# Both feed-forward networks of a hybrid block: the down projection two tiles behind the up projection, ScalarE's copy with fewer waits, and the running sum of squares on GpSimd

## The chip, the cores and the metric

The kernel runs on one core of one Trainium2 chip. The core has TensorE (PE) for matmuls, VectorE (DVE) and ScalarE (ACT) for elementwise work, GpSimd (POOL), and SyncE (SP), which here only issues transfers. Each engine runs its own instructions in the order in which they are written and waits for the others through semaphores. The metric is the device time of one execution in microseconds, as the median of several runs.

## The reference, cut to what matters

The whole block is four residual steps on `x` of 8 x 512 rows by 256 columns: attention, a feed-forward network (FFN), a recurrent scan, and the same FFN once more with the same weights. The FFN is this:

```
def _ternary_linear(x, w):
    alpha = jnp.mean(jnp.abs(w))
    w_t = jnp.sign(w) * (jnp.abs(w) > 0.5 * alpha).astype(w.dtype)
    rms = jnp.sqrt(jnp.sum(x * x, axis=-1, keepdims=True)) / jnp.sqrt(x.shape[-1])
    return jnp.einsum('bsd,fd->bsf', x / (rms + 1e-8), w_t)     # (forward value)

h = jax.nn.gelu(_ternary_linear(layernorm(x), w_up), approximate=False)    # 256 -> 1024
x = x + _ternary_linear(h, w_down)                                         # 1024 -> 256
```

So each FFN needs gelu of an up projection, the down projection of that, and for each row the sum of the squares of its 1024 values of `h`, by which the result is scaled.

## The kernel before, in words

`x` stays in SBUF through all four steps. An FFN (`ffn_pe`, `ffn_act`, `ffn_dve`, `ffn_pool`, one function for each engine, called with i = 0 for the first FFN and i = 1 for the second) goes over 8 **batches** q of 512 rows. Within a batch it goes over NF = 8 **tiles** n of 128 hidden features; t = 8q + n numbers all tiles. All of an FFN's matrices of one tile are 128 partitions (features) by 512 columns (rows of x).

For one tile t these steps are done:

- TensorE, `up` (L267): 4 matmuls of 512 columns, fp16 weights with the high and the low half of `x` (`xh`), into PSUM bank 2 or 3 in turn. It waits until ScalarE's gelu of tile t-2 has read that bank (semaphore `g`).
- ScalarE: gelu from the bank into `h` (L322, fp32, two buffers), a copy scaled by 2^7 and rounded to fp16 into `hh[..., 0]` (L327), and the square into `hsq` (L328, two buffers). Before the gelu it waits for `up` of t, and for VectorE's low half of t-2 (`hl`), which reads `h`. Before the copy it waits for the down projection of t-2 (`dnm`), whose `hh` buffer it writes, and for the sum that reads the `hsq` buffer (`ss`); the square comes after the copy.
- VectorE: the low half `hh[..., 1]` = h * 2^7 - hh[..., 0] (L413), and from n = 1 on, the running sum of squares `ssq` (L425, 7 additions a batch).
- TensorE, `down` (L282): 8 matmuls of 256 columns with `hh` of both halves as weights, which add up in PSUM over the 8 tiles.

TensorE's order within a batch is up(t), down(t-1), up(t+1), down(t), and so on. `square_sums` (L291: 8 passes of a matmul against a column of ones) of batch q-1 follows at n = 1, and the transposes of the next batch's rows (`turned_rows`, L240) at n = 2 and 3.

VectorE has, beside L413 and L425, work for the neighbouring batches, written out by hand tile by tile: at n = 0 the scales and the normalised rows of the next batch (L357 to L367), at n = 1 to 3 the layernorm statistics of the batch after it (L343 to L353), at n = 4 and 5 the low half of the next `xh` (L251), at n = 2 the reading of the square sums of the batch before (L373), at n = 4 the scale from them (L377, L379), at n = 4 to 6 the residual additions (L386), and in the first FFN at n = 6 and 7 the statistics for the layernorm of the scan (L394 to L403). GpSimd takes only small powers: the root of the square sums (`output_roots`, L465), the roots of the variances (`row_roots`, L255), and once in the first FFN L478.

SyncE's queue stores each finished batch in the second FFN (L532), after `x` is complete.

Of the kernel before, what the change touches and what calls it, by code (L numbers as in the profile page):

```python
# [34 lines left out]
P = 128  # L35
# [49 lines left out]
def build(nc, a_in, out):  # L85
    with ExitStack() as ctx:
# [3 lines left out]
        def sb(name, shape, dt=F32, where=ctx):  # L90
            return where.enter_context(nc.sbuf_tensor(name, shape, dt))
# [65 lines left out]
        mid.close()  # L157
        xh = sb("xh", [P, 2, 2, KD, L], F16, mid)
        h = sb("h", [P, 2, L], F32, mid)
        hh = sb("hh", [P, 2, 2, L], F16, mid)  # L160
        hsq = sb("hsq", [P, 2, L], F32, mid)
        ssq = sb("ssq", [P, 3, L], F32, mid)
        ysc = sb("ysc", [P, 4, NT], F32, mid)
# [93 lines left out]
        def ffn_pe(pe, i):  # L257
            def up(q, n):
                t = q * NF + n
                if n == 0:  # L260
                    pe.wait_ge(F["hi"], q * KD + KD)
                    pe.wait_ge(F["lo"], q * KD + KD)
                if t >= 2:
                    pe.wait_ge(F["g"], t - 1)
                for part in range(2):
                    for k in range(KD):
                        last = pe.matmul(bank[2 + n % 2][:, :], wup[:, k, n * P:(n + 1) * P], xh[:, q % 2, part, k, :],  # L267
                                         start=(part == 0 and k == 0), stop=(part == 1 and k == KD - 1))
                last.then_inc(F["up"], 1)

            def down(t):
                q, e = divmod(t, NF)
                pe.wait_ge(F["hh"], t + 1)
                pe.wait_ge(F["hl"], t + 1)
                if e == 0 and q >= 2:
                    pe.wait_ge(F["x"], (q - 1) * NT)
                if e == 0 and q in (B, B + 1):
                    pe.wait_ge(O["t"], (2 * NT - 1) * B - 2 * (B + 1 - q))
                    pe.wait_ge(Z["sq"], B - 2 * (B + 1 - q))
                for u in range(NT):  # L280
                    for part in range(2):
                        last = pe.matmul(bank[4 + q % 2 * 2 + u // 2][:, u % 2 * D:u % 2 * D + D],  # L282
                                         hh[:, t % 2, part, u * P:(u + 1) * P], wdn[:, e, :],
                                         start=(e == 0 and part == 0 and u % 2 == 0), stop=(e == NF - 1 and part == 1),
                                         skip_group_check=True)
                last.then_inc(F["dnm"], 1)

            def square_sums(q):
                pe.wait_ge(F["ss"], q * (NF - 1) + NF - 1)
                for u in range(NT):  # L290
                    last = pe.matmul(bank[0][:, u:u + 1], ssq[:, (q * (NF - 1) + NF - 2) % 3, u * P:(u + 1) * P], ones[:, 0:1],  # L291
                                     start=True, stop=True, skip_group_check=True)
                last.then_inc(F["sm"], 1)

            if i == 0:
                pe.wait_ge(w_q, 2)
                pe.wait_ge(A["x2"], B * NT)
                for k in (1, 0):
                    turned_rows(pe, 0, k)
            for q in range(i * B, i * B + B):  # L300
                for n in range(NF):
                    up(q, n)
                    if q > i * B or n > 0:
                        down(q * NF + n - 1)
                    if n == 1 and q > i * B:
                        square_sums(q - 1)
                    if n in (2, 3) and q < i * B + B - 1:
                        turned_rows(pe, q + 1, 3 - n)
            down((i * B + B) * NF - 1)
            square_sums(i * B + B - 1)  # L310

        def ffn_act(act, i):
            if i == 0:
                for k in (1, 0):
                    high_half(act, 0, k)
            for q in range(i * B, i * B + B):
                for n in range(NF):
                    t = q * NF + n
                    act.wait_ge(F["up"], t + 1)
                    if t >= 2:  # L320
                        act.wait_ge(F["hl"], t - 1)
                    act.activation(h[:, t % 2, :], bank[2 + n % 2][:, :], ACT.Gelu, scale=1.0 / HI_X).then_inc(F["g"], 1)  # L322
                    act.wait_ge(F["g"], t + 1)
                    if t >= 2:
                        act.wait_ge(F["dnm"], t - 1)
                        act.wait_ge(F["ss"], q * (NF - 1) + max(n - 2, min(n, 2) - 1))
                    act.activation(hh[:, t % 2, 0, :], h[:, t % 2, :], ACT.Copy, scale=HI_H).then_inc(F["hh"], 1)  # L327
                    act.activation(hsq[:, t % 2, :], h[:, t % 2, :], ACT.Square).then_inc(F["sq"], 1)  # L328
                    if n in (3, 4) and q < i * B + B - 1:
                        high_half(act, q + 1, 4 - n)  # L330
# [39 lines left out]
        def ffn_dve(dve, i):  # L370
# [38 lines left out]
            for q in range(q0, q9 + 1):  # L409
                for n in range(NF):  # L410
                    t = q * NF + n
                    dve.wait_ge(F["hh"], t + 1)
                    dve.scalar_tensor_tensor(hh[:, t % 2, 1, :], h[:, t % 2, :], HI_H, hh[:, t % 2, 0, :],  # L413
                                             ALU.mult, ALU.subtract).then_inc(F["hl"], 1)
                    if n >= 1:
                        s = q * (NF - 1) + n - 1
                        dve.wait_ge(F["sq"], t + 1)
                        if n == 1:
                            old = hsq[:, 1 - t % 2, :]
                        else:  # L420
                            old = ssq[:, (s - 1) % 3, :]
                            dve.wait_ge(F["ss"], s)
                        if n == 3:
                            dve.wait_ge(F["sm"], q)
                        dve.tensor_tensor(ssq[:, s % 3, :], old, hsq[:, t % 2, :], ALU.add).then_inc(F["ss"], 1)  # L425
                    if i == 0 and n == 0 and q == 3:
                        dve.wait_ge(C["mc"], 2)
                        dve.tensor_scalar(tile_columns(0), mean_b[:, 0:B * NT:NT, 1], LN_EPS, None, ALU.add).then_inc(C["ve"], 1)
                    if i == 0 and n == 0 and q == 5:
                        dve.wait_ge(C["rs"], 1)  # L430
                        dve.scalar_tensor_tensor(tile_columns(2), mean_b[:, 0:B * NT:NT, 0], -1.0, tile_columns(1),
                                                 ALU.mult, ALU.mult).then_inc(C["nm"], 1)
                    if q < q9:
                        if n == 0:
                            row_scales(dve, q + 1)
                            rows_normalised(dve, q + 1, range(NT))
                        if n in (4, 5):
                            low_half(dve, q + 1, 5 - n)
                    if q + 1 < q9:
                        if n in (1, 2):  # L440
                            row_stats(dve, q + 2, (2 * n - 2, 2 * n - 1))
                        if n == 3:
                            row_moments(dve, q + 2)
                    if q > q0:
                        if n == 2:
                            read_sums(q - 1)
                        if n == 4:
                            output_scales(q - 1)
                        if n in (4, 5, 6):
                            add_rows(q - 1, ((0,), (1, 2), (3,))[n - 4])  # L450
                        if i == 0 and n in (6, 7):
                            next_stats(q - 1, (2 * n - 12, 2 * n - 11))
                        if i == 0 and n == 7:
                            next_moments(q - 1)
# [7 lines left out]
        def ffn_pool(pool, i):  # L462
            def output_roots(q):
                pool.wait_ge(F["sr"], q + 1)
                pool.tensor_tensor(ysc[:, 1, :], ysc[:, 0, :], halves[:, 0, :], ALU.pow).then_inc(F["s1"], 1)  # L465
# [3 lines left out]
                row_roots(pool, 0)  # L469
                row_roots(pool, 1)  # L470
            for q in range(q0, q9 + 1):
                if q > q0:
                    output_roots(q - 1)
                if q + 1 < q9:
                    row_roots(pool, q + 2)
                if i == 0 and q == 3:
                    pool.wait_ge(C["ve"], 1)
                    pool.tensor_tensor(tile_columns(1), tile_columns(0), inverse[:, :, 0], ALU.pow).then_inc(C["rs"], 1)  # L478
            output_roots(q9)

        block = ctx.enter_context(nc.Block())
# [1400 lines left out]
```

## Time and profile before

| | value |
|---|---|
| median of 3 runs | 2365.93 us (2363.47 to 2369.75) |
| the profiled execution: time, span | 2368.05 us, 2366.3 us |
| granted TensorE clock, mean over the span | 0.836 of full |
| busy share of the span: PE, DVE, ACT, POOL | 77%, 89%, 70%, 40% |
| first FFN: first `up` to last reading of the square sums | 488.4 to 645.7 us |
| second FFN: the same | 2206.3 to 2359.6 us |

The two FFNs stand at the two ends of the recurrent scan, in which VectorE is busy nearly all of the time. An FFN's time is best read as a period: L373 runs once a batch, so the distance from one L373 to the next is the time of one batch of 8 tiles. Durations of a row contain a tail during which the next instruction of the same engine already runs; the distance from start to start says what an instruction costs its engine.

### The profile page before, as it was taken

Reading aid. Unit: us, or ns where it says so; the run is one execution under the profiler, and the core shown is the slowest. Engines: PE = TensorE matmul, PEld = TensorE weight load, DVE = VectorE, ACT = ScalarE, POOL = GpSimd, SP = SyncE. Lnnn points to the kernel's source line nnn. Section 1 sums busy time; section 2 is a strip of 40 time slices with the busy share of each in tenths; the row PEclk is TensorE's granted clock in tenths of the full one; section 3 lists DMA queues with packets and bytes.
Section 4 is the critical chain, followed back from the end, with each engine's and each line's share of the span. In section 5 each row is a group of like instructions: output and inputs, shape, how many; then the busy total and the mean of one; then the engine's idle time right before and its main releaser. Section 6 shows DMA issues by size and latency. Waiting matters only on the chain.

```text
span 2366.3 us, 47628 instructions
## 1 busy us (share of the span) xinstructions
PE 1824.5 (77%) x12321; PEld 1478.2 (62%) x12321; DVE 2117.0 (89%) x9102; ACT 1656.0 (70%) x5481; POOL 956.6 (40%) x1608
## 2 busy tenths in 40 slices
PE   5888888788888777877777788877877877343887
PEld 3555555455587666777777777777766777342654
DVE  6888777679817999999999999999999999999887
ACT  4878888667746666667777777777777666555776
POOL 0000000001005666666665666666666555666110
PEclk8999899889997888788888777888778777666999
DMA  6000000000000000000000000000000000000001
GB/s 189 18 18 22 18 18 18 13 1 1 1 1 1 1 1 1 1 1 1 2 1 1 1 1 2 1 1 1 1 1 1 1 1 1 1 1 1 10 28 36
DMA packets 14351, 25.00 MB, mean 11 GB/s; under 512 B 1280, under 2 KB 12032, under 8 KB 13824
## 3 DMA queue, kind: packets, MB, share of 16 engines
q1 hardware_dynamic: 14080, 21.97, 3.2%
q8 instruction: 99, 1.62, 0.3%
q14 instruction: 172, 1.41, 0.2%
HBM read 12.27 MB, written 4.19 MB: 7 GB/s over the span
## 4 chain that ended last, share of the span: by engine, by line
DVE 63%; PE 14%; issue 13%; ACT 5%; POOL 0%; DVEq 0%; POOLq 0%; ACTq 0%
DVE xs L1581 9%; DVE pn L1561 8%; DVE bank L1565 8%; DVE U L1630 7%; DVE bank L1595 7%; DVE pn L1586 6%; DVE kv L1619 5%; PE bank L282 3%; PE bank L267 3%; ACT prob L923 2%; PE bank L585 2%; DVE bank L1603 2%; DVE bank L1615 1%; PE bank L632 1%; PE bank L669 1%
## 5 line engine op out<-in xcount | busy, mean ns | idle before, releaser
L750 PE MATMUL bank<-U,ident 128*128 128x128 f32 x2048 | 463.5, 398 | 159.6 <-ACT go L1064 140.1
L750 PEld LDWEIGHTS bank<-U,ident 128*128 128x128 f32 x2048 | 430.1, 257 | 195.5 <-issue 162.3
L1779 POOL TENSOR_TENSOR wu<-U,stg 128x256 f32<-128x256 f32 x512 | 317.7, 620 | 561.3 <-DVE U L1630 561.3
L1253 ACT ACTIVATE xs<-U 128x128 f32<-128x128 f32 x1024 | 261.4, 301 | 304.1 <-DVE U L1630 301.4
L761 PE MATMUL bank<-stack,tm 128*128 128x64 f32 x1792 | 273.8, 324 | 110.1 <-ACT tm L994 100.4
L761 PEld LDWEIGHTS bank<-stack,tm 128*128 128x128 f32 x1792 | 263.7, 237 | 127.5 <-ACT tm L994 115.8
L1708 POOL TENSOR_TENSOR kv<-stg 128x256 f32<-128x256 f32 x513 | 317.4, 619 | 0.0
L1581 DVE TENSOR_TENSOR xs<-U,bank 128x128 f32<-128x128 f32 x1024 | 243.5, 278 | 62.1 <-ACT bank L1107 61.1
L1565 DVE TENSOR_TENSOR bank<-wu,bank 128x128 f32<-128x128 f32 x1024 | 290.0, 283 | 1.8 <-POOL wu L1779 1.4
L735 PE MATMUL bank<-wcat,yT 128*128 128x224 f32 x1024 | 275.9, 425 | 5.8 <-issue 5.4
L1595 DVE TENSOR_TENSOR bank<-pn,bank 128x128 f32<-128x128 f32 x1024 | 248.3, 288 | 1.1 <-issue 0.8
L1630 DVE TENSOR_TENSOR U<-bank,kv 128x128 f32<-128x128 f32 x1024 | 246.6, 281 | 2.4 <-issue 1.7
L735 PEld LDWEIGHTS bank<-wcat,yT 128*128 128x128 f32 x1024 | 228.0, 233 | 28.4 <-issue 18.8
L1561 DVE TENSOR_REDUCE pn<-xs 128x8 f32<-128x128 f32 x1026 | 241.0, 275 | 0.2 <-ACT xs L1253 0.2
L1586 DVE TENSOR_REDUCE pn<-xs 128x8 f32<-128x128 f32 x1024 | 238.9, 274 | 0.0
L923 ACT ACTIVATE prob<-bank,nmax 128x128 f32<-128x128 f32 x512 | 180.5, 371 | 48.7 <-DVE nmax L1369 48.1
L282 PE MATMUL bank<-wdn,hh 128*128 128x256 f16 x1024 | 133.3, 273 | 41.0 <-DVE hh L413 31.3
L1155 ACT ACTIVATE small<-pn 128x16 f32<-128x16 f32 x513 | 110.8, 216 | 75.2 <-DVE pn L1561 33.0
L1619 DVE TENSOR_TENSOR kv<-bank,kv 128x256 f32<-128x256 f32 x384 | 159.6, 416 | 0.5
L994 ACT ACTIVATE tm<-bank 64x448 f32<-64x448 f32 x256 | 136.0, 531 | 32.8 <-PE bank L761 27.1
L282 PEld LDWEIGHTS bank<-wdn,hh 128*128 128x128 f16 x1024 | 92.9, 97 | 102.2 <-issue 64.2
L1369 DVE TENSOR_REDUCE nmax<-bank 128x4 f32<-128x512 f32 x128 | 87.7, 685 | 67.7 <-PE bank L620 67.2
(213 smaller groups left out, 3708.0 us busy)
## 6 DMA issues: line engine op xcount, KB each, us to landing
out_x<-x SPq DMA_DIRECT2D x8, 512.0 KB, 2.9
x<-in_x SPq DMA_DIRECT2D x1, 3584.0 KB, 16.9
Vs<-V SPq DMA_DIRECT2D x8, 384.0 KB, 4.6
Vs<-V SPq DMA_DIRECT2D x8, 288.0 KB, 3.3
lane<-in_lanes SPq DMA_DIRECT2D x8, 256.0 KB, 3.2
wcat<-in_wcat SPq DMA_DIRECT2D x1, 1792.0 KB, 14.5
wraw<-in_w_up SPq DMA_DIRECT2D x1, 1024.0 KB, 19.0
wraw<-in_w_down SPq DMA_DIRECT2D x1, 1024.0 KB, 11.4
```

Of the source, the lines that this page charges most:

```text
L282: last = pe.matmul(bank[4 + q % 2 * 2 + u // 2][:, u % 2 * D:u % 2 * D + D], hh[:, t % 2, part, u * P:(u + 1) * P], wdn[:, e, :], start=(e ...
L735: last = pe.matmul(bank[dst][:, e * PB * H:(e + 1) * PB * H], yT[:, (pc // 2) % 2, k, pc % 2, 4 * g + 2 * e:4 * g + 2 * e + 2, :].rearrang ...
L750: last = pe.matmul(rsum.rearrange("p (t i) -> p t i", i=HD), ident[:, :], steps[:, :, :, j], start=(j == 0), stop=(j == HD - 1))
L761: last = pe.matmul(bank[3 + g][:, e * CH:(e + 1) * CH], tm[:, g * (PB // 2) + e, :, :].rearrange("p a c -> p (a c)"), stack[:, :], start=T ...
L1561: dve.tensor_reduce(pn[:, e, 1, :], ij(xs[:, e, 1, :]), AXX, ALU.add).then_inc(S["ps"], 1)
L1565: dve.tensor_tensor(rows8(zz, e), rows8(wu, e), rows8(zz, e), ALU.subtract).then_inc(T[e]["d"], 1)
L1581: dve.tensor_tensor(ij(xs[:, e, 0, :]), ij(rows8(U[:, half if j else 1 - half, (j - 1) % STEPS, :], e)), row(kkr[:, jj, :], i=HD // 2), AL ...
L1586: dve.tensor_reduce(pn[:, e, 0, :], ij(xs[:, e, 0, :]), AXX, ALU.add).then_inc(T[e]["pn"], 1)
L1595: dve.tensor_tensor(ij(rows8(zz, e)), col(pn[:, e, 0, :], HD // 2), row(kkar[:, g, jj, :], i=HD // 2), ALU.mult).then_inc(T[e]["z"], 1)
L1630: dve.tensor_tensor(rows8(U[:, half, j, :], e), rows8(zz, e), rows8(new, e), ALU.add).then_inc(T[e]["u"], 1)
L1708: pool.tensor_tensor(ij(kv0[:, j % 2, :]), col(stg[:, half, j, TK, :]), row(stg[:, half, j, TV, :]), ALU.mult).then_inc(S["k0"], 1)
L1779: pool.tensor_tensor(ij(wu[:, :]), ij(U[:, half if j else 1 - half, (j - 1) % STEPS, :]), col(stg[:, half, j, TW, :]), ALU.mult).then_inc( ...
```

## The change

The down projection runs two tiles behind the up projection instead of one; `hh` gets a third buffer for it. On ScalarE the copy waits for the down projection of t-3 instead of t-2, and the wait for the running sum moves from before the copy to before the square. The 7 additions a batch that keep the running sum leave VectorE and go to GpSimd, with their waits; GpSimd's roots, which stood at the head of each batch, now follow its additions of n = 3, 5 and 6.

```
-        hh = sb("hh", [P, 2, 2, L], F16, mid)
+        hh = sb("hh", [P, 3, 2, L], F16, mid)
 ... ffn_pe (and hh[:, t % 3 ...] in down)
                     up(q, n)
-                    if q > i * B or n > 0:
-                        down(q * NF + n - 1)
+                    if q > i * B or n > 1:
+                        down(q * NF + n - 2)
 ...
-            down((i * B + B) * NF - 1)
+            for t in (2, 1):
+                down((i * B + B) * NF - t)
             square_sums(i * B + B - 1)
 ... ffn_act
                     if t >= 2:
-                        act.wait_ge(F["dnm"], t - 1)
+                        act.wait_ge(F["dnm"], t - 2)
+                    act.activation(hh[:, t % 3, 0, :], h[:, t % 2, :], ACT.Copy, scale=HI_H).then_inc(F["hh"], 1)
+                    if t >= 2:
                         act.wait_ge(F["ss"], q * (NF - 1) + max(n - 2, min(n, 2) - 1))
-                    act.activation(hh[:, t % 2, 0, :], h[:, t % 2, :], ACT.Copy, scale=HI_H).then_inc(F["hh"], 1)
                     act.activation(hsq[:, t % 2, :], h[:, t % 2, :], ACT.Square).then_inc(F["sq"], 1)
 ... ffn_dve: the block "if n >= 1: ... tensor_tensor(ssq ...)" is gone
 ... ffn_pool
             for q in range(q0, q9 + 1):
-                if q > q0:
-                    output_roots(q - 1)
-                if q + 1 < q9:
-                    row_roots(pool, q + 2)
-                if i == 0 and q == 3:
-                    (L478)
+                for n in range(1, NF):
+                    s = q * (NF - 1) + n - 1
+                    t = q * NF + n
+                    pool.wait_ge(F["sq"], t + 1)
+                    if n == 1:
+                        old = hsq[:, 1 - t % 2, :]
+                    else:
+                        old = ssq[:, (s - 1) % 3, :]
+                        pool.wait_ge(F["ss"], s)
+                    if n == 3:
+                        pool.wait_ge(F["sm"], q)
+                    pool.tensor_tensor(ssq[:, s % 3, :], old, hsq[:, t % 2, :], ALU.add).then_inc(F["ss"], 1)
+                    if n == 3 and q > q0:
+                        output_roots(q - 1)
+                    if n == 5 and q + 1 < q9:
+                        row_roots(pool, q + 2)
+                    if n == 6 and i == 0 and q == 3:
+                        (L478)
```

## Rows read from the trace of the kernel before

**Rows 1.** One batch of each FFN: window, busy by engine (instructions), clock, DMA share, GB/s

```profile
core 0: us, PE busy (x) PEld busy (x) DVE busy (x) ACT busy (x) POOL busy (x), PEclk, DMA share, GB/s
...
555.43:575.31 19.88, 16.82 (x113) 10.54 (x112) 18.08 (x53) 15.01 (x27) 4.55 (x3) 1.00 0.00 1
...
2254.00:2273.00 19.00, 16.56 (x112) 10.61 (x112) 16.20 (x44) 14.76 (x27) 2.64 (x2) 1.00 0.09 29
```

**Rows 2.** Line L373, once a batch: count, duration ns, first and last start

```profile
L373 DVE TENSOR_SCALAR ysc<-bank x16: 143/144/162, 515.7 to 2359.6; 128x4 f32<-128x4 f32 x16
...
L373 DVE TENSOR_SCALAR ysc<-bank x1: 154/154/154, 633.9 to 633.9; 128x4 f32<-128x4 f32 x1
...
L373 DVE TENSOR_SCALAR ysc<-bank x1: 144/144/144, 2234.9 to 2234.9; 128x4 f32<-128x4 f32 x1
...
L373 DVE TENSOR_SCALAR ysc<-bank x1: 154/154/154, 2347.9 to 2347.9; 128x4 f32<-128x4 f32 x1
```

**Rows 3.** Timeline, one tile round in batch 0: start, us, engine, line [idle before]

```profile
503.59 0.60 ACT L322 ACTIVATE h<-bank 128x512 f32<-128x512 f32 x1
...
504.21 0.63 ACT L327 ACTIVATE hh<-h 128x512 f16<-128x512 f32 x1
...
504.75 0.61 ACT L328 ACTIVATE hsq<-h 128x512 f32<-128x512 f32 x1
504.88 0.69 DVE L413 SCALAR_TENSOR_TENSOR hh<-h,hh 128x512 f16<-128x512 f32 x1
...
505.72 1.03 PE L282 MATMUL bank<-wdn,hh 128*128 128x256 f16 x8
...
506.59 1.03 PE L267 MATMUL bank<-xh,wup 128*128 128x512 f16 x4
...
507.65 0.60 ACT L322 ACTIVATE h<-bank 128x512 f32<-128x512 f32 x1
```

**Rows 4.** Waits in the first FFN: who, for whom: us, times, longest

```profile
PEld bank L282 <- issue: 38.7, 49, 1.5
ACT h L322 <- PE bank L267: 33.3, 44, 1.9
...
DVE hh L413 <- ACT hh L327: 19.9, 28, 3.3
```

**Rows 5.** Chain of waits, TensorE back to back at a batch's start: start, us, what

```profile
570.44 0.79 PE bank L291 x8
571.23 0.89 PE bank L267 x4
572.11 0.88 PE bank L282 x8
572.99 0.44 PE bank L240 x4
```

**Rows 6.** Timeline of VectorE over tiles n = 0 and 1 of a batch

```profile
568.62 0.68 DVE L413 SCALAR_TENSOR_TENSOR hh<-h,hh 128x512 f16<-128x512 f32 x1
...
571.12 0.68 DVE L413 SCALAR_TENSOR_TENSOR hh<-h,hh 128x512 f16<-128x512 f32 x1
...
571.72 0.68 DVE L425 TENSOR_TENSOR ssq<-hsq 128x512 f32<-128x512 f32 x1
...
572.32 0.74 DVE L343 BATCH_NORM_STATS2 st<-x 128x6 f32<-128x256 f32 x2
```

**Rows 7.** GpSimd by shape, whole span: count, busy us, mean ns, idle before

```profile
L1731 POOL TENSOR_TENSOR ov<-rs,fac 128x128 f32<-128x128 f32 x65 | 29.6, 456 | 0.8 <-ACT fac L1145 0.8
...
L255 POOL TENSOR_TENSOR sd<-vv,halves 128x8 f32<-128x8 f32 x16 | 26.2, 1638 | 195.4 <-DVE vv L353 195.4
...
L1746 POOL TENSOR_TENSOR y<-y,ln_w 128x256 f32<-128x256 f32 x24 | 17.4, 725 | 0.4 <-ACT y L1099 0.4
...
L465 POOL TENSOR_TENSOR ysc<-ysc,halves 128x4 f32<-128x4 f32 x16 | 16.1, 1007 | 239.3 <-DVE ysc L373 239.3
```

**Rows 8.** Timeline, a GpSimd root and VectorE's low half at the same time

```profile
500.59 1.64 POOL L255 TENSOR_TENSOR sd<-vv,halves 128x8 f32<-128x8 f32 x1 [17.35 <-DVE vv L353]
...
500.81 0.69 DVE L413 SCALAR_TENSOR_TENSOR hh<-h,hh 128x512 f16<-128x512 f32 x1 [0.30 <-ACT hh L327]
```

More of the change, by code:

```diff
@@ L282, in down @@
                         last = pe.matmul(bank[4 + q % 2 * 2 + u // 2][:, u % 2 * D:u % 2 * D + D],
-                                         hh[:, t % 2, part, u * P:(u + 1) * P], wdn[:, e, :],
+                                         hh[:, t % 3, part, u * P:(u + 1) * P], wdn[:, e, :],
                                          start=(e == 0 and part == 0 and u % 2 == 0), stop=(e == NF - 1 and part == 1),
@@ L412, in ffn_dve @@
                     dve.wait_ge(F["hh"], t + 1)
-                    dve.scalar_tensor_tensor(hh[:, t % 2, 1, :], h[:, t % 2, :], HI_H, hh[:, t % 2, 0, :],
+                    dve.scalar_tensor_tensor(hh[:, t % 3, 1, :], h[:, t % 2, :], HI_H, hh[:, t % 3, 0, :],
                                              ALU.mult, ALU.subtract).then_inc(F["hl"], 1)
[L415 to L425, printed above, removed]
                     if i == 0 and n == 0 and q == 3:
@@ L471, in ffn_pool @@
             for q in range(q0, q9 + 1):
-                if q > q0:
-                    output_roots(q - 1)
-                if q + 1 < q9:
-                    row_roots(pool, q + 2)
-                if i == 0 and q == 3:
-                    pool.wait_ge(C["ve"], 1)
-                    pool.tensor_tensor(tile_columns(1), tile_columns(0), inverse[:, :, 0], ALU.pow).then_inc(C["rs"], 1)
+                for n in range(1, NF):
[15 more added lines that the diff above has]
+                    if n == 6 and i == 0 and q == 3:
+                        pool.wait_ge(C["ve"], 1)
+                        pool.tensor_tensor(tile_columns(1), tile_columns(0), inverse[:, :, 0], ALU.pow).then_inc(C["rs"], 1)
             output_roots(q9)
```

## The prediction

> **What bounds the kernel now.** I read the page's slices first: the two FFNs are short stages in which all of TensorE, VectorE and ScalarE are at six to nine tenths, so a share of busy time names no bound there. The next view is the busy time by window over exactly one batch, from one L373 to the next [rows 1]. In the first FFN a batch takes 19.88 us, VectorE is busy for 18.08 of them, TensorE for 16.82, ScalarE for 15.01. In the second it takes 19.00 us with VectorE at 16.20. So VectorE is nearly the bound in the first FFN and not in the second, which is hardly faster: something else holds both. The granted clock is 1.00 in both windows, which is the 2.4 GHz level.
>
> The starts of L373 [rows 2] give the mean period: from 515.7 to 633.9 are six batches, 19.7 us each; from 2234.9 to 2347.9 six batches, 18.83 us each.
>
> The timeline of one round shows the second limit [rows 3]. Gelu of tile t starts at 503.59, the copy at 504.21, VectorE's low half at 504.88, the down projection at 505.72, the up projection behind it at 506.59, and only when that is done at 507.62 can the gelu of t+2 start, at 507.65. That is a loop over four engines of 4.06 us for two tiles, 2.03 us a tile, 16.2 us for eight, with every engine idle in part of it. The view of waits says the same [rows 4]: ScalarE's gelu waits 33.3 us for the up projection, VectorE's low half 19.9 us for the copy, and TensorE stands 38.7 us ahead of the down projection. On top of the loop come VectorE's bursts: L413 of n = 0 and that of n = 1 are 2.50 us apart (568.62, 571.12) because the next batch's rows are normalised in between, and L425 follows every one of them [rows 6]. So a batch is partly the loop, partly VectorE's queue in front of L413.
>
> **The floor of each engine after the change.** TensorE: an up projection costs 0.87 us from start to start, a down projection 0.88 (572.11 to 572.99, 505.72 to 506.59), the square sums 0.79, one group of transposes 0.44 [rows 3, 5]. 8 x 1.75 + 0.79 + 2 x 0.44 = 15.7 us a batch. ScalarE issues what it issued, 15.0 us busy [rows 1], and waits for less. VectorE loses 7 additions at 0.60 us from start to start (571.72 to 572.32 [rows 6]), 4.2 us a batch: 18.1 becomes 13.9 in the first FFN, 16.2 becomes 12.0 in the second. GpSimd gains 7 additions of 128x512 from two inputs. The trace has none of that size, so it is extrapolated: 456 ns for 128 columns, 725 for 256 [rows 7], 2.1 ns a column, so 1.26 us for 512. From below the cost is 0.725 us (the 256-column row itself), from above 2.5 us, twice the extrapolation, if something on the way halves its rate. I take 1.26, and 1.33 with the wait of each addition for the one before it, an estimate of 0.07 from the gaps between the rows of [rows 3] (the low half starts 0.04 us after the copy ends). 7 x 1.33 + 1.01 + 1.64 = 12.0 us a batch, under TensorE's 15.7. TensorE is then the bound.
>
> **What each wait is worth then.** *Down two behind.* In TensorE's order, 3.5 us pass (two ups and two downs) between the end of up(t), where gelu(t) starts, and down(t). The low half of t ends 1.98 us after the gelu's start (503.59 to 505.57 [rows 3]), and 0.15 us later the matmul starts (505.72). The slack is 3.5 - 2.1 = 1.4 us, where before it was negative (0.88 + 0.87 - 2.1). The loop over the four engines now spans three tiles for its 2.1 + 0.9 + 1.0 = 4.0 us, 1.35 us a tile, and falls away behind TensorE's 1.75. What is late next is VectorE's queue: at n = 0 the 2.5 us burst delays L413 of n = 1 by about 2.5 - 1.75 = 0.75 us, inside the slack. In the first FFN n = 4 to 7 hold the residual additions and two sets of statistics and come to about 2 us each, so 4 x 0.25 = 1.0 us of delay runs into the burst and makes 1.75, beyond the slack by 0.35. I add 0.4 us a batch there and nothing in the second FFN.
>
> *The copy's waits.* Both waits before the copy hardly cost anything before: the list of waits in the first FFN has one of 0.5 us, in the second none. No gain. The square now carries the wait for the sum of t-2, and behind it on ScalarE stand the next gelu and so the next up projection. With the addition ending 1.16 + 0.61 + 0.08 + 1.26 = 3.1 us after gelu(t) [rows 3, 7] and the square of t+2 starting 3.5 + 1.16 = 4.7 us after it, there is 1.6 us of room. The two roots take it: additions 3, 4, 5, 6 run back to back with 1.01 and 1.64 us between them. 4 x 1.33 + 2.65 + 1.85 = 9.8 us after gelu(3), the sum of n = 6 is done, and the square of the next batch's n = 0 wants it 5 x 1.75 + 1.16 = 9.9 us after gelu(3). That is an even fit, so I add 0.3 us a batch for it in both FFNs; if an addition took 1.5 us it would be 0.7 more.
>
> *Square sums.* TensorE reaches them after down(7) of the batch before, 3.5 + 0.88 us after gelu(7); by the same count the last addition of the batch, behind the roots, ends at 9.8 + 1.33 = 11.1 us after gelu(3), that is 4.1 us after gelu(7). It fits by 0.3 us, and what it costs if not is the whole of the overrun on TensorE's queue. L478 adds 1.9 us once. GpSimd's roots come later than before but VectorE wants L465's result at n = 4 and L255's only in the next batch. SyncE's stores in the second FFN come closer together; they are 0.09 of the DMA engines' time [rows 1], nothing waits for them but the last, which follows the end as before.
>
> **The sum.** A batch comes to 15.7 + 0.4 + 0.3 = 16.4 us in the first FFN and 16.0 in the second. Between the L373 of [rows 2]: 6 x (19.7 - 16.4) = 19.8 us and 6 x (18.83 - 16.0) = 17.0 us. Before the first L373 of an FFN lie ten tiles more, at the loop's 2.03 us a tile: 10 x (2.03 - 1.75) = 2.8 us, of which I take 2.5 for each FFN, 5.0 together. Behind the last one lie five tiles, 1.4 us, less 0.2 at the very end, where the square sums now wait for square and addition (3.1 us after the gelu, and 0.1 for the wait) and not for low half and down (2.13 + 0.88 = 3.0 us): 1.0 with a little lost, 2.0 together. The gain is 19.8 + 17.0 + 5.0 + 2.0 = 43.8 us. The profiled execution took 2368.05 us (span 2366.3 and 1.75 around it), so 2324.2; the median of the runs shown is 2.1 us lower, and I forecast **2323 us**. With every added loss at nothing it would be 15.7 us a batch and about 2314.
>
> **Where VectorE and GpSimd may meet.** Overlap of a large GpSimd operation with a VectorE operation that reads two tensors in SBUF is a resource that the trace shows only in small: L413 reads `h` and `hh`, both in SBUF, and ran from 500.81 for 0.69 us inside a GpSimd root (500.59 for 1.64 us), neither longer than elsewhere [rows 8]. That is the nearest row and I take nothing for it; but the root reads 8 columns and the addition 1024.
>
> The Trainium skill says otherwise ("SBUF — State Buffer", section "Who interferes with whom"): a VectorE instruction with two SBUF inputs and a GpSimd instruction that reads SBUF exclude each other, and whichever issues first holds the pair for its whole length. By that rule L413 of [rows 8] should have started at 502.23; it did not, so for a whole instruction the trace disagrees, but a narrower form of it (while the operands stream) would be open. By it the time would be that of the first rival, 2343 us.
>
> **Rivals.** *1. Low half and addition take turns (0.33).* What it does here: each of the 8 low halves (0.66 us) and 7 additions (1.26) a batch runs alone, with some 0.1 us for each handing over. Lowest sum: 5.3 + 8.8 + 1.5 = 15.6, just TensorE's floor; but VectorE also has 9.1 us of other work a batch in the first FFN (13.9 - 8 x 0.60), and when it comes late to L413 it finds GpSimd inside an addition. In strict turns a tile costs 0.66 + 1.26 + 0.2 = 2.1 us where there is an addition, and n = 0 2.5: 7 x 2.1 + 2.5 = 17.2, and the root's delays bring it to 17.8 in the first FFN, say 17.4 in the second. Gain 6 x 1.9 + 6 x 1.4 + 4 = 24 us: 2368 - 24 - 2 = 2342, say 2343. For it: the addition fills its operands' path for over a microsecond. Against it: [rows 8].
>
> *2. The other side: GpSimd becomes the bound (0.07).* ScalarE's square waits for the addition of t-2, so everything goes at GpSimd's pace once 7 additions and 2.65 us of roots exceed the old period, 7a + 2.65 > 19.2, a > 2.4 us. It decides from there; at 3 us an addition a batch takes 23.7 us and 14 of them cost 4.4 us each, about 60 us, 2425. For it: the extrapolation is from half the width, and VectorE's queue may slow it. Against it: the two widths of [rows 7] put it at half of that.
>
> *3. The period hardly moves (0.07).* The wait for the sums, or another wait before TensorE, takes the place of the loop and a batch stays at 18.5 to 19.5 us: 2355 to 2368, around 2360. For it: four engines between 75 and 100% have little room for each other. Against: no single count above gives over 16.4.
>
> **How the numbers follow.** The forecast, 2314 to 2332, has 0.53, rival 1 (2334 to 2352) 0.33, rival 3 0.07, rival 2 0.07. A measurement of this kernel tells from no change what is over 0.3%, 7 us. Faster: 0.53 + 0.33 and a small part of rival 3, 0.87. Same: 0.06. Slower: 0.07. The range, 2311 to 2351, leaves out rivals 2 and 3 and a little of each end.
>
> **What would show it.** After: no VectorE addition in the FFNs; GpSimd's addition at 1.2 to 1.35 us; the period of L373 near 16.4 and 16.0 us with TensorE's busy time at 15.7 or more of it and no wait over 0.5 us ahead of L282; the gelu waiting for the up projection only. Rival 1 shows as additions and L413 longer than 1.35 and 0.69 us, or starting only when the other ends. Rival 2 shows as ScalarE's square waiting for GpSimd at most tiles. The scan between the FFNs should keep its length to some microseconds; if the whole differs while the FFNs' periods come out as said, the reason lies there. The prediction is wrong if the period stays above 18 us, or if the square sums hold TensorE.

## The result, and the profile after

The changed kernel takes 2353.66 us (median of 6 runs, 2348.46 to 2361.97), the kernel before beside it 2368.14 us (median of 6). The ratio is 0.9942 with a 95% interval of 0.9920 to 0.9964: some 14 us faster. The forecast was 2323 us with a range of 2311 to 2351; the sign was right, the gain was a third of it, and the time lies above the range.

The profiled execution took 2354.65 us (span 2352.5). First, the same two windows of one batch each as in [rows 1] (window, then busy us and instructions of PE, PEld, DVE, ACT, POOL, the granted clock, DMA):

```profile
core 0: us, PE busy (x) PEld busy (x) DVE busy (x) ACT busy (x) POOL busy (x), PEclk, DMA share, GB/s
550.30:570.50 20.20, 16.41 (x112) 10.91 (x112) 18.73 (x47) 15.36 (x29) 14.17 (x11) 1.00 0.00 1
2245.50:2263.90 18.40, 16.25 (x112) 10.99 (x112) 16.54 (x37) 14.58 (x27) 12.65 (x10) 1.00 0.09 30
```

VectorE has 6 or 7 instructions fewer in each window and is busier than before in both (18.73 against 18.08 us, 16.54 against 16.20). Single batches mislead here, though: the first window holds the one batch with L481, GpSimd's extra power, and at 20.2 us it is the longest of the first FFN. Over six batches of each FFN the picture is milder; the first two rows are from the kernel before, the last two from the changed one:

```profile
515.70:633.90 118.20, 99.08 (x664) 62.50 (x665) 103.42 (x294) 88.72 (x157) 16.13 (x12) 1.00 0.00 1
2234.90:2347.90 113.00, 98.08 (x664) 62.85 (x664) 92.40 (x231) 88.48 (x157) 14.22 (x11) 1.00 0.09 29
...
512.60:621.30 108.70, 97.94 (x675) 65.77 (x674) 95.65 (x252) 87.36 (x157) 74.33 (x55) 1.00 0.00 1
2227.20:2332.40 105.20, 95.85 (x664) 65.22 (x665) 90.37 (x190) 85.12 (x154) 72.92 (x53) 1.00 0.09 31
```

The 42 additions that left VectorE were 28.6 us of its busy time in six batches, and VectorE is less busy by only 7.8 us in the first FFN and 2.0 in the second: most of what was taken from it came back as longer instructions. The reading of the square sums, L375 after the change, gives the periods (count, duration ns, first and last start):

```profile
L375 DVE TENSOR_SCALAR ysc<-bank x16: 135/139/163, 512.6 to 2345.8; 128x4 f32<-128x4 f32 x16
...
L375 DVE TENSOR_SCALAR ysc<-bank x1: 153/153/153, 621.3 to 621.3; 128x4 f32<-128x4 f32 x1
...
L375 DVE TENSOR_SCALAR ysc<-bank x1: 136/136/136, 2227.2 to 2227.2; 128x4 f32<-128x4 f32 x1
...
L375 DVE TENSOR_SCALAR ysc<-bank x1: 155/155/155, 2332.4 to 2332.4; 128x4 f32<-128x4 f32 x1
```

Six batches from 512.6 to 621.3 are 18.1 us each (19.7 before [rows 2]), six from 2227.2 to 2332.4 are 17.5 (18.83 before). That is 9.5 and 7.8 us gained. The first FFN starts its first up projection at 486.9 and the second at 2197.1; before its first L375 the first FFN needs 25.7 us (27.3 before) and the second 30.1 (28.6 before), and behind the last period each needs 13.4 us (11.8 before). So the ends give 3.2 us back, and 14 us are left. The granted clock has a part in the starts: it was 0.50, the 1.2 GHz level, from 2211.4 to 2214.8 us before and from 2205.1 to 2208.5 after, and in the changed kernel once more from 508.7 to 512.1. An up projection that takes 1.03 us at full clock takes 1.91 us there (at 2206.38).

The timeline shows why the batches are longer than forecast. These are rows of one batch of the first FFN, the longest one (start, us, engine, line):

```profile
564.66 2.34 DVE L369 TENSOR_SCALAR xn<-x,mv,rstd 128x256 f32<-128x256 f32 x4
564.93 1.27 POOL L474 TENSOR_TENSOR ssq<-hsq 128x512 f32<-128x512 f32 x1 [0.74 <-ACT hsq L330]
...
568.08 1.26 POOL L474 TENSOR_TENSOR ssq<-ssq,hsq 128x512 f32<-128x512 f32 x1 [1.88 <-ACT hsq L330]
568.19 1.70 DVE L415 SCALAR_TENSOR_TENSOR hh<-h,hh 128x512 f16<-128x512 f32 x1
...
576.05 0.68 DVE L415 SCALAR_TENSOR_TENSOR hh<-h,hh 128x512 f16<-128x512 f32 x1
576.26 1.61 POOL L474 TENSOR_TENSOR ssq<-ssq,hsq 128x512 f32<-128x512 f32 x1 [0.88 <-ACT hsq L330]
```

At 568.08 GpSimd starts an addition and ends it at 569.34. VectorE's low half, which takes 0.69 us alone, comes 0.11 us after it, takes 1.70 us and ends at 569.89, 0.55 us after the addition. At 576.05 it is the other way round: the low half is first and keeps its 0.68 us, and the addition takes 1.61 us in place of 1.27 and ends 1.14 us after it. Who comes second waits. The four normalised rows, 1.38 us before, take 2.34 with an addition among them; this meets one of the six batches between the readings of the first FFN and every batch but one of the second. Of the 128 low halves 27 take over 1 us. Over the first FFN, by line and shape (count, busy us, mean ns, idle before):

```profile
L415 DVE SCALAR_TENSOR_TENSOR hh<-h,hh 128x512 f16<-128x512 f32 x64 | 53.2, 834 | 20.3 <-ACT hh L327 20.3
...
L379 DVE TENSOR_SCALAR ysc<-ysc 128x4 f32<-128x4 f32 x8 | 5.4, 676 | 2.0 <-POOL ysc L456 2.0
...
L361 DVE RECIPROCAL rstd<-den 128x4 f32<-128x4 f32 x7 | 1.2, 178 | 0.2
...
L474 POOL TENSOR_TENSOR ssq<-ssq,hsq 128x512 f32<-128x512 f32 x48 | 67.1, 1397 | 36.0 <-ACT hsq L330 34.7
```

L379 is a scaling of 4 columns, 0.16 us before, and takes 0.68 on the mean; the reciprocal L361 of the same size is untouched. So it is not VectorE as a whole that slows, but certain instructions. GpSimd's additions pay as well: 1.40 us on the mean, with a median of 1.27. What TensorE waited for in the six periods of the first FFN is the third view (who, for whom: us, times, longest):

```profile
PEld bank L240 <- DVE xn L369: 4.4, 5, 1.1
PEld bank L240 <- issue: 4.2, 4, 1.5
PEld bank L291 <- POOL ssq L474: 3.4, 5, 2.2
...
PE bank L282 <- DVE hh L415: 2.6, 5, 0.6
```

The wait before the down projection, which was the largest before [rows 4], has largely gone; in its place stand the transposes, which wait for normalised rows that come late (blocked themselves in one batch, in others behind a blocked scaling such as L363, 0.91 to 0.95 us in place of 0.17), and the square sums, which wait for a delayed addition.

### The profile page after: what moved, and what is told of

It is laid out like the page before. It is cut to its first block, busy times and chain, and to the rows that moved or that the text cites. A ratio compares the mean times of both kernels' runs of the same rounds, so it can differ in the third digit from the quotient of the medians.

```text
span 2352.5 us, 47628 instructions
## 1 busy us (share of the span) xinstructions
PE 1836.6 (78%) x12321; PEld 1498.5 (64%) x12321; DVE 2104.1 (89%) x8990; ACT 1652.0 (70%) x5481; POOL 1116.6 (47%) x1720
## 4 chain that ended last, share of the span: by engine, by line
DVE 63%; issue 14%; PE 11%; ACT 5%; POOL 2%; DVEq 0%; POOLq 0%; ACTq 0%
DVE xs L1584 9%; DVE pn L1564 8%; DVE bank L1568 8%; DVE U L1633 7%; DVE bank L1598 7%; DVE pn L1589 6%; DVE kv L1622 5%; ACT prob L926 2%; PE bank L588 2%; PE bank L267 2%; DVE bank L1606 2%; POOL ssq L474 2%; DVE bank L1618 1%; PE bank L282 1%; PE bank L635 1%
## 5 line engine op out<-in xcount | busy, mean ns | idle before, releaser
L764 PE MATMUL bank<-stack,tm 128*128 128x64 f32 x1792 | 279.7, 329 | 109.6 <-ACT tm L997 100.9
L764 PEld LDWEIGHTS bank<-stack,tm 128*128 128x128 f32 x1792 | 269.4, 241 | 126.6 <-ACT tm L997 116.2
L738 PE MATMUL bank<-wcat,yT 128*128 128x224 f32 x1024 | 286.8, 438 | 8.2 <-issue 7.7
L738 PEld LDWEIGHTS bank<-wcat,yT 128*128 128x128 f32 x1024 | 236.5, 241 | 33.1 <-issue 21.6
L474 POOL TENSOR_TENSOR ssq<-ssq,hsq 128x512 f32<-128x512 f32 x96 | 133.4, 1390 | 75.8 <-ACT hsq L330 73.1
L415 DVE SCALAR_TENSOR_TENSOR hh<-h,hh 128x512 f16<-128x512 f32 x128 | 110.9, 868 | 41.3 <-ACT hh L327 41.3
## 6 DMA issues: line engine op xcount, KB each, us to landing
x<-in_x SPq DMA_DIRECT2D x1, 3584.0 KB, 16.9
```

The source lines that it names most:

```text
L738: last = pe.matmul(bank[dst][:, e * PB * H:(e + 1) * PB * H], yT[:, (pc // 2) % 2, k, pc % 2, 4 * g + 2 * e:4 * g + 2 * e + 2, :].rearrang ...
L764: last = pe.matmul(bank[3 + g][:, e * CH:(e + 1) * CH], tm[:, g * (PB // 2) + e, :, :].rearrange("p a c -> p (a c)"), stack[:, :], start=T ...
```

## The experiments

Theory 1: VectorE's low half and GpSimd's addition take turns, which the prediction had as its first rival, and this ate the gain. Theory 2: the new order or the freed VectorE is worth less than was worked out, with no exclusion needed. Theory 3: GpSimd is late with its row of additions and roots, whatever they read. Kernels that did not run together are compared below by their ratios to the kernel before, each against its own runs of it; 0.001 is 2.4 us, the intervals are 3.5 to 5.5 us to either side, and a difference between two changed kernels is uncertain by some 5 to 8 us. Rows are of one profiled execution each.

**The order alone.** The down projection two behind, with VectorE keeping the sums.

```
 ... ffn_dve, after the low half
+                    if n >= 1:
+                        dve.wait_ge(F["sq"], t + 1)
+                        ...
+                        dve.tensor_tensor(ssq[:, s % 3, :], old, hsq[:, t % 2, :], ALU.add).then_inc(F["ss"], 1)
 ... ffn_pool
-                    pool.tensor_tensor(ssq[:, s % 3, :], old, hsq[:, t % 2, :], ALU.add).then_inc(F["ss"], 1)
```

> Only the order is changed: the down projection two tiles behind, the third buffer, and the copy freed, as in the changed kernel, but VectorE keeps the running sums as before. Theory 1 (VectorE's low half and GpSimd's addition exclude each other, and that ate the gain): no large GpSimd work is left, so L413 keeps its 0.69 us. VectorE's own 18.1 us a batch bound the first FFN at about 18.3 us, TensorE and bursts the second at about 16.5: 6 x 1.4 + 6 x 2.3 + 4 = 26 us less than before, about 2341 us, faster than the changed kernel's 2353.7. Theory 2 (the order gains little by itself, because VectorE's bursts are what TensorE waits for, and the changed kernel's gain came from the work moved to GpSimd): about 2360 us, slower than the changed kernel.

Measured: 2343.22 us, ratio to before 0.9886 (0.9863 to 0.9909), so 13 us better than the change as a whole. The windows of one batch each, and then of six:

```profile
core 0: us, PE busy (x) PEld busy (x) DVE busy (x) ACT busy (x) POOL busy (x), PEclk, DMA share, GB/s
549.30:568.60 19.30, 16.32 (x112) 10.70 (x112) 17.78 (x53) 14.58 (x27) 5.65 (x3) 1.00 0.00 1
2256.20:2273.50 17.30, 15.94 (x112) 10.88 (x112) 15.94 (x43) 14.72 (x27) 3.59 (x2) 1.00 0.09 32
...
510.30:623.10 112.80, 97.45 (x669) 63.99 (x670) 102.45 (x293) 86.91 (x156) 21.02 (x12) 1.00 0.00 1
2221.60:2323.10 101.50, 94.98 (x669) 65.09 (x670) 91.18 (x232) 87.53 (x156) 18.97 (x11) 1.00 0.10 32
```

The total came as theory 1 had it, though the batches were slower than I wrote: the last two rows, six batches each, give means of 18.8 and 16.9 us, against 18.3 and 16.5. In the first FFN a batch is only 0.9 us shorter than before, with VectorE busy for 102.5 of 112.8 us.

The changed kernel does not lose its 13 us to this one in the batches. Its six batches of the first FFN are shorter than here (108.7 us against 112.8) and those of the second longer (105.2 against 101.5), which together is level: in the batches what VectorE was relieved of and what the blocked instructions cost weigh the same. Of the 12.2 us between the two profiled executions 11.5 lie at the FFNs' ends: there the changed kernel takes 25.7 and 30.1 us to the first reading against 24.4 and 25.0 here, and 13.4 us twice behind the last period against 11.2 and 10.5. A part of it is the clock, which stands at 1.00 in the window to the first reading of the second FFN here (2196.6 to 2221.6) and at 0.94 in the changed kernel (2197.1 to 2227.2), where TensorE first waited 2.7 us for the normalised rows.

GpSimd shows the exclusion from its side. Its root of 4 columns follows L375 at once, where VectorE's low half and addition stand:

```profile
L467 POOL TENSOR_TENSOR ysc<-ysc,halves x16: 1006/1987/1990, 510.5 to 2333.8; 128x4 f32<-128x4 f32 x16
```

Its median is 1.99 us, against 1.01 before [rows 7].

**The sums alone.** GpSimd adds, but the down projection stays one tile behind, with two buffers.

```
-        hh = sb("hh", [P, 3, 2, L], F16, mid)
+        hh = sb("hh", [P, 2, 2, L], F16, mid)
-                    if q > i * B or n > 1:
-                        down(q * NF + n - 2)
+                    if q > i * B or n > 0:
+                        down(q * NF + n - 1)
-                        act.wait_ge(F["dnm"], t - 2)
+                        act.wait_ge(F["dnm"], t - 1)
```

> Only the sums are moved to GpSimd; the down projection stays one tile behind, hh keeps two buffers. Theory 1: each blocked low half (up to 1.76 us in place of 0.69) stands inside the loop gelu, copy, low half, down, up, which has no slack, so this is worse than before or level: a batch at 19.5 to 20.5 us, 2365 to 2380 us. Theory 2 (relief of VectorE is what gains): a batch near the loop's 16.2 us plus bursts, about 17.5, 2342 us.

Measured: 2361.47 us, ratio 0.9966 (0.9950 to 0.9982). Neither theory gave this number: it is a small gain where theory 1 had a loss or no change and theory 2 a gain of 26 us. The low halves are blocked (first FFN: 779 ns on the mean), but less than in the changed kernel (834): 17 of 128 take over 1 us here, 27 there. With the loop still closed VectorE may come to the low half as soon as the copy is done and so before the addition; that was not tried by itself. Order and sums together give 14 us, less than the 27 of the order alone: the sums on GpSimd are a gain of 8 us (4 to either side) in the old order and a loss of 13 (8 to either side) in the new.

**Without additions.** They are left out on all engines; the square sums are taken over ones, so the scale of the result is left out.

```
-                    pool.tensor_tensor(ssq[:, s % 3, :], old, hsq[:, t % 2, :], ALU.add).then_inc(F["ss"], 1)
+                    if q == q0 and n == 1:
+                        pool.memset(ssq[:, :, :], 1.0).then_inc(F["ss"], 1)
 ... ffn_pe
-                pe.wait_ge(F["ss"], q * (NF - 1) + NF - 1)
+                pe.wait_ge(F["sq"], q * NF + NF)
+                pe.wait_ge(F["ss"], q // B + 1)
 ... ffn_act: the wait for F["ss"] is gone
```

> The changed kernel without the additions on any engine (the square sums are taken over ones, so the scale of the result is left out; a single GpSimd memset an FFN fills the tile). It shows what the order and the freed VectorE give when nothing is paid on GpSimd. Theory 1: L415 back at 0.69 us, the period at TensorE's 15.7 to 16.4 us, about 2368 - 44 = 2324 us, the number of the forecast. Theory 2 (a floor of its own in the order, such as the transposes behind the normalised rows): the period stays over 17 us, 2340 us or more.

Measured: 2315.58 us, ratio 0.9783 (0.9761 to 0.9805). The windows over six batches of each FFN:

```profile
core 0: us, PE busy (x) PEld busy (x) DVE busy (x) ACT busy (x) POOL busy (x), PEclk, DMA share, GB/s
510.70:604.70 94.00, 93.50 (x667) 65.59 (x666) 78.02 (x251) 85.75 (x157) 16.15 (x12) 1.00 0.01 1
2202.60:2295.40 92.80, 92.80 (x668) 65.66 (x667) 68.28 (x190) 85.47 (x157) 14.22 (x11) 1.00 0.11 35
```

15.7 and 15.5 us a batch with TensorE busy throughout: the floor of the prediction (15.7), reached. Theory 2 falls.

**GpSimd busy, but only writing.** Each addition becomes two memsets in the same place with the same waits and signals; the running sum is left out.

```
-                    pool.tensor_tensor(ssq[:, s % 3, :], old, hsq[:, t % 2, :], ALU.add).then_inc(F["ss"], 1)
+                    pool.memset(filler[:, :], 0.0)
+                    pool.memset(ssq[:, s % 3, :], 1.0).then_inc(F["ss"], 1)
```

> The changed kernel with each of GpSimd's additions replaced by two memsets (768 and 512 columns), same place, same waits and signals: GpSimd only writes, and is busy for about as long (0.9 to 1.5 us a tile, to be read from the trace). The running sum is left out. Theory 1 (the exclusion is between VectorE's second SBUF input and GpSimd's reads): L415 back at 0.69 us and the period at 15.9 to 16.6 us, about 2325 us. Theory 3 (GpSimd is simply late: its roots and additions in a row hold the square and the square sums, whatever they read): no change from the changed kernel, a period near 18 us and about 2350 us, with L415 at 0.69 us all the same or blocked if any GpSimd work blocks it.

Measured: 2328.36 us, ratio 0.9827 (0.9807 to 0.9847). Lines L472 and L473 are GpSimd's memsets in the first FFN, L416 is the low half and L370 the normalised rows over the whole span (min/median/max ns):

```profile
L472 POOL MEMSET filler<- 128x768 f32 x56 | 41.3, 738 | 54.1 <-ACT hsq L331 53.4
L473 POOL MEMSET ssq<- 128x512 f32 x56 | 30.5, 545 | 0.0
...
L416 DVE SCALAR_TENSOR_TENSOR hh<-h,hh x128: 666/684/720, 491.2 to 2319.4; 128x512 f16<-128x512 f32 x128
...
L370 DVE TENSOR_SCALAR xn<-x,mv,rstd x64: 394/410/1010, 476.5 to 2293.2; 128x256 f32<-128x256 f32 x64
```

GpSimd is busy for 1.28 us a tile, as long as an addition, and the low half is free (720 ns at most). The changed kernel stands 38 us above the kernel without additions; 27 of them are gone. So what blocks the low half is that GpSimd reads, and theory 3 explains little. But the normalised rows are still blocked, up to 1.01 us, by writes alone, and some 10 us remain (7 to either side). In the profiled executions most of that lies in the first FFN, whose six batches take 101.2 us against 94.0 without additions, while those of the second take 93.5 against 92.8. Not all of it is blocking: the granted clock was at half from 560.2 to 563.6 us, inside the first FFN's batches, and from 2198.6 to 2202.0 in the second FFN's start; without additions there is no such stretch at either place. The Trainium skill has both halves of this ("SBUF — State Buffer", section "Who interferes with whom"): an instruction with two SBUF inputs contends with GpSimd's reads only, a `tensor_scalar` or copy that can run over two ports contends with any GpSimd access. For the low half and the `tensor_scalar` the rows agree, except that L370 shows no doubled rate (0.345 us from start to start for 256 columns, where the low half takes 0.60 for 512) and is blocked all the same. No row here shows a copy that was blocked.

**One input in PSUM.** GpSimd adds at full width; the gelu stays in the up projection's PSUM bank, so the low half reads one tensor in SBUF.

```
-                    act.activation(h[:, t % 2, :], bank[2 + n % 2][:, :], ACT.Gelu, scale=1.0 / HI_X).then_inc(F["g"], 1)
+                    act.activation(bank[2 + n % 2][:, :], bank[2 + n % 2][:, :], ACT.Gelu, scale=1.0 / HI_X).then_inc(F["g"], 1)
 ... copy and square read bank[2 + n % 2] too
-                    dve.wait_ge(F["hh"], t + 1)
-                    dve.scalar_tensor_tensor(hh[:, t % 3, 1, :], h[:, t % 2, :], HI_H, hh[:, t % 3, 0, :],
+                    dve.wait_ge(F["sq"], t + 1)
+                    dve.scalar_tensor_tensor(hh[:, t % 3, 1, :], bank[2 + n % 2][:, :], HI_H, hh[:, t % 3, 0, :],
 ... ffn_pe, up
-                    pe.wait_ge(F["g"], t - 1)
+                    pe.wait_ge(F["hl"], t - 1)
```

> GpSimd adds as in the changed kernel, but the gelu writes h in place into the up projection's PSUM bank, so that VectorE's low half reads only one tensor in SBUF. For that the low half waits for the square, and the up projection of t+2 waits for the low half of t, which is 2.5 us after the gelu against 2.6 us until TensorE gets there. Theory 1 (the low half is blocked because it has two SBUF inputs while GpSimd reads): L415 never over 0.75 us, though GpSimd's additions stay at full width; the normalised rows L369 stay blocked. The period then is 16.5 to 17.5 us (new coupling included), 2330 to 2345 us. If anything else makes L415 long (any overlap with GpSimd), its longest instances stay near 1.7 us and the time at 2350 us or more.

Measured: 2336.35 us, ratio 0.9856 (0.9839 to 0.9873), 20 us better than the change. L413 is the low half over the whole span, L472 the addition and L367 the normalised rows in the first FFN:

```profile
L413 DVE SCALAR_TENSOR_TENSOR hh<-bank,hh x128: 665/691/693, 489.5 to 2326.3; 128x512 f16<-128x512 f32 x128
...
L472 POOL TENSOR_TENSOR ssq<-ssq,hsq 128x512 f32<-128x512 f32 x42 | 53.2, 1268 | 29.5 <-ACT hsq L328 28.8
...
L367 DVE TENSOR_SCALAR xn<-x,mv,rstd 128x256 f32<-128x256 f32 x28 | 16.4, 647 | 0.3
```

128 low halves beside GpSimd's additions, none over 693 ns, and the additions at 1268. Besides the memory of one operand the waits were changed, but not so that the two would miss each other: the low half waits for the square as the addition does, and they start together (548.16 and 548.20, 0.69 and 1.27 us long). This is the strongest evidence for theory 1. The normalised rows pay as before (647 ns on the mean), and the up projection now waits for the low half, so this kernel is not at the floor.

**Half the length.** The additions cover 256 columns; the other half of the sums is left out.

```
-                    pool.tensor_tensor(ssq[:, s % 3, :], old, hsq[:, t % 2, :], ALU.add).then_inc(F["ss"], 1)
+                    pool.tensor_tensor(ssq[:, s % 3, 0:L // 2], old, hsq[:, t % 2, 0:L // 2], ALU.add).then_inc(F["ss"], 1)
```

> The changed kernel with GpSimd's additions over 256 of the 512 columns; the other half of the sums is left out (ones in its place). It gives the price by length. Theory 1: an addition takes 0.73 us, a blocked low half at most 0.69 + 0.73 us, and about half of the way from the changed kernel (2353.7) to the kernel without additions (2315.6) or a little more is won, for the shorter addition is also met less often: 2328 to 2335 us. If the cost were for each GpSimd instruction and not by its length (the semaphores, the order of the roots), it would stay within 5 us of 2353.7.

Measured: 2323.74 us, ratio 0.9797 (0.9782 to 0.9812), just under the range that I gave theory 1. The longest low half is 1209 ns (1757 in the changed kernel over the whole span), the addition 776 on the mean, with a median of 728:

```profile
L416 DVE SCALAR_TENSOR_TENSOR hh<-h,hh x128: 667/691/1209, 491.3 to 2312.5; 128x512 f16<-128x512 f32 x128
...
L477 POOL TENSOR_TENSOR ssq<-ssq,hsq 128x256 f32<-128x256 f32 x44 | 34.1, 776 | 44.4 <-ACT hsq L331 44.4
```

Half of the length takes away 34 of the 38 us (6 to either side): the cost goes by length, but is not proportional to it. Probably a wait of 0.5 us fits into the slack that the two-behind order gives and one of 1.1 us does not; and a shorter addition is met less often, 3 low halves over 1 us instead of 27. No run tells these two apart.

**A version that beats both.** VectorE keeps the sums in the new order, in fp16 throughout.

```
-        hsq = sb("hsq", [P, 2, L], F32, mid)
-        ssq = sb("ssq", [P, 3, L], F32, mid)
+        hsq = sb("hsq", [P, 2, L], F16, mid)
+        ssq = sb("ssq", [P, 3, L], F16, mid)
 ... square_sums
-                    ... ones[:, 0:1],
+                    ... onesh[:, 0:1],
```

> As the run with VectorE's sums and the down projection two behind, but squares, running sum and the column of ones are fp16. Nothing large is left on GpSimd. If an fp16 addition of 512 columns costs half of the fp32 one (0.33 us from start to start in place of 0.60), VectorE loses 1.9 us a batch: first FFN from 19.3 to about 17 us, second from 17.3 to about 16.2 us, and the square sums on TensorE get shorter by some 0.3 us; 2343 - 13 - 7 - 3 = 2320 us. If the fp16 addition is no faster, about 2341 us.

Measured: 2324.37 us, ratio 0.9811 (0.9797 to 0.9825), 46 us under the kernel before beside it (2370.65). The addition (L428, first FFN) and the windows of one batch each:

```profile
L428 DVE TENSOR_TENSOR ssq<-ssq,hsq 128x512 f16<-128x512 f16 x42 | 17.5, 418 | 0.1
```

```profile
core 0: us, PE busy (x) PEld busy (x) DVE busy (x) ACT busy (x) POOL busy (x), PEclk, DMA share, GB/s
546.50:564.30 17.80, 15.65 (x108) 10.05 (x108) 16.01 (x54) 14.55 (x27) 5.05 (x3) 1.00 0.00 1
2227.30:2243.20 15.90, 15.10 (x108) 10.25 (x108) 14.14 (x43) 14.44 (x27) 3.33 (x2) 1.00 0.10 35
```

These windows are again of the longer batches. By the starts of the reading of the square sums (L376 here), six batches are 17.2 us each in the first FFN and 15.5 in the second, which is at the level of the kernel without additions; the first FFN stays above it with VectorE's own work. From start to start the fp16 addition costs 0.34 us, where I had expected 0.33. The price is that squares and running sum are rounded to fp16.

## Why the prediction was wrong

- *The bound before* was read rightly: with the additions gone from every engine the new order gives 15.7 and 15.5 us a batch, and TensorE is busy for 93.5 of 94.0 and 92.8 of 92.8 us, so that the waits before the down projection are gone.
- *The floor of TensorE*, 15.7 us, was measured to a tenth. The 0.4 us for VectorE's bursts was not seen in the kernel without additions. The 0.3 for the roots can only be read where GpSimd is busy: with memsets as long as the additions the second FFN takes 15.6 us a batch, so it was not seen there either. Together they are 6 us of the 8 by which the kernel without additions is under the forecast. (2324.2 less 2.1 is 2322.1 and not 2323; that changes nothing.)
- *The length of the addition* was right: 1.26 us worked out from two widths, 1.27 the median.
- *The step that failed* is "That is the nearest row and I take nothing for it", about VectorE and GpSimd meeting. [rows 8] shows a low half that passes unharmed through a GpSimd root, but such a root reads 8 columns, and it stood for an operation that reads 1024. In the changed kernel too low halves pass through roots unharmed (0.68 us at 539.53, inside the root from 539.33 to 540.97), and 27 are held by additions for up to 1.1 us. My reading is that the two exclude each other only while operands are read, and that little of the root's 1.64 us is reading; the runs do not test that by itself. The term taken at nothing measured up to 38 us (changed kernel against the one without additions). The runs put the reads at some 27 of them (changed kernel against memsets; 20 by the kernel with h in PSUM, which has a new wait of its own) and the rest at 10; blocked `tensor_scalar` instructions fit this rest, and so does a granted clock at half in two stretches, and neither was tried by itself.
- *Where it was missed.* The forecast gain of 43.8 us had 36.8 in the six periods of each FFN and 7.0 at the ends. Measured were 17.3 and a loss of 3.2. Without additions the ends gain 8.3 us, so their term was sound too and was lost to the same step: in the second FFN's start transposes wait 2.7 us for blocked normalised rows, and behind the last period of each FFN two or three low halves are held (1290, 973 and 1101 ns from 627.65 on). The period of the first FFN, 18.1 us, is over the 18 that the prediction named as a sign of being wrong.
- *Rival 1* was the true mechanism and its size was off too: it had 17.8 and 17.4 us a batch, measured were 18.1 and 17.5, and it had the FFNs' ends 4 us shorter where they came out 3 us longer. Its sign, additions over 1.35 us and low halves over 0.69, is in the rows; its 2343 us is 11 too low. It counted only the low half as blocked. The normalised rows and the scalings, which read one tensor from SBUF, were in no case of the prediction, nor was a fall of the granted clock.
- *The copy's waits* were priced at nothing, and no run contradicts that; none changes them alone. *Square sums fit by 0.3 us* failed in the changed kernel (L291 waited up to 2.2 us) because additions were delayed; with memsets of the same length it waited 2.1 us in the first FFN in all.
- *The scan between* kept its length: 1560.5 us from the last reading of one FFN to the first up projection of the next before, 1562.4 after.

The range failed with it: it ended at 2351 for a rival whose price had a missing term.

## What to carry to other kernels

Before work is moved from VectorE to GpSimd, list which VectorE instructions it will run beside: in these traces those with two SBUF inputs (against its reads) and `tensor_scalar` from SBUF to SBUF take turns with it. Those with one input in PSUM (L388: 484 ns at most, 474 the median), the statistics (L345: 428 at most, 409 the median), the reciprocal (L361: 179 at most), and the scan's reductions (L1561 in the kernel before: 285 at most of 1026, 275 the median) don't. An overlap with a tiny GpSimd operation in the trace proves nothing for one that reads much. Where VectorE is the bound, a cheaper form of the instruction (here fp16, 0.34 for 0.60 us from start to start) may be worth more than another engine, and each half of a double change deserves its own run: here one half was worth 27 us alone and the other took 13 of them back. A gain should be read over several periods, and at a stage's two ends apart from them: here a single batch and the mean of six told different stories, and the ends a third.

## What the runs showed of the hardware that was not expected

- A GpSimd write (memset) delays VectorE's `tensor_scalar` of 256 columns (1010 ns at most, 410 the median) and even of 4 columns (median 559 ns against 158 before), and leaves an instruction with two SBUF inputs alone (720 ns at most).
- VectorE delays GpSimd too: a power of 4 columns takes 1.99 us (median) in place of 1.01 when it starts beside low half and addition, though a power that is already running does not hold a low half.
- GpSimd's cost by width in these traces: additions 0.73 us for 256 columns and 1.27 for 512 (medians); memsets 0.55 us for 512 and 0.74 for 768.
